# Attention scores, row maxima, window masks and layer-norm means issued as four column tiles of 32

## The reference, cut to what matters

```python
# layer 0, per image b, 4 heads of 16 channels
x_ln   = layernorm(x)                        # over the 64 channels
q,k,v  = split(einsum(x_ln, qkv_w))
scores = einsum(q, k) / sqrt(16)             # 1024 x 1024 per head
out    = softmax(scores) @ v
x      = x + proj(out)
x      = x + fc2(gelu(fc1(layernorm(x))))
# layer 1, per image, 8 heads of 64 channels, each token sees a window of 32 tokens
dot    = einsum(q1, windows_of(k1))
t      = t + softmax(dot) @ windows_of(v1) @ Wu
t      = t + scan(sigmoid(batchnorm(layernorm(t) @ W) + y @ V.T))
```

## Time and profile before

| what | us |
|---|---|
| median of 3 runs (lowest to highest) | 453.4 (451.02 to 453.89) |
| the profiled execution | 450.95 |
| its span, first to last instruction | 449.2 |
| PE busy, DVE busy, ACT busy | 410.0, 296.0, 296.4 |
| mean granted TensorE clock | 0.983 of 2.4 GHz |

### The profile page before, as it was taken

The page is one execution under the profiler, slowest core; times in us unless marked ns, Lnnn a source line. Parts: engine busy times, 40 slices in busy tenths (PEclk is TensorE's granted clock), DMA queues, the critical chain, the costliest instruction groups (busy, mean ns, idle before and its releaser), DMA issues.

```text
span 449.2 us, 7886 instructions
## 1 busy us (share of the span) xinstructions
PE 410.0 (91%) x3207; PEld 155.4 (35%) x3207; DVE 296.0 (66%) x541; ACT 296.4 (66%) x512; POOL 40.7 (9%) x55
## 2 busy tenths in 40 slices
PE   7789999999999999999999999899999888897893
PEld 2334323223223433333223333232234322453492
DVE  2698978989997646689986447996142635625424
ACT  3534777768786675796785684878976666164551
POOL 9100300002021000030040000000300001100000
PEclk9998999999999999999999999999999999699997
DMA  8400280004600000007200000000000000000003
GB/s 307 92 1 3 50 161 14 0 14 105 107 2 10 4 1 3 9 6 166 47 0 13 1 1 3 12 2 3 1 3 1 0 1 0 3 1 2 1 1 95
DMA packets 6942, 14.02 MB, mean 31 GB/s; under 512 B 1528, under 2 KB 4088, under 8 KB 6776
## 3 DMA queue, kind: packets, MB, share of 16 engines
q1 hardware_dynamic: 6760, 13.36, 12.7%
q10 hardware_dynamic: 144, 0.14, 0.1%
HBM read 9.20 MB, written 3.41 MB: 28 GB/s over the span
## 4 chain that ended last, share of the span: by engine, by line
PE 66%; ACT 18%; DVE 12%; issue 3%; DVEq 0%; ACTq 0%
PE O L828 11%; PE T L813 6%; DVE part_max L1318 5%; ACT z L1182 5%; PE T L793 5%; PE R L813 4%; ACT probs L1159 4%; PE R L793 4%; PE R L997 3%; PE R L958 3%; PE R L718 3%; PE R L724 3%; PE R L884 2%; PE R L985 2%; PE R L972 2%
## 5 line engine op out<-in xcount | busy, mean ns | idle before, releaser
L1318 DVE TENSOR_REDUCE part_max<-T 128x1 f32<-128x512 f32 x160 | 103.1, 681 | 16.7 <-PE T L793 16.3
L1159 ACT ACTIVATE probs<-T 128x512 f32<-128x512 f32 x151 | 84.4, 599 | 20.7 <-PE T L813 20.2
L1159 ACT ACTIVATE probs<-R 128x512 f32<-128x512 f32 x105 | 59.5, 601 | 20.1 <-PE R L813 19.5
L828 PE MATMUL O<-probs,VT 128*32 128x512 f32 x512 | 67.8, 603 | 0.4 <-ACT probs L1159 0.3
L1318 DVE TENSOR_REDUCE part_max<-R 128x1 f32<-128x512 f32 x96 | 62.8, 681 | 4.6 <-PE R L793 4.4
L793 PE MATMUL T<-KX,QX 96*128 96x512 bf16 x160 | 55.0, 387 | 4.4 <-DVE part_max L1318 2.1
L813 PE MATMUL T<-QX,KX 99*128 99x512 bf16 x151 | 51.8, 383 | 2.3 <-DVE part_max L1318 2.3
L813 PE MATMUL R<-QX,KX 99*128 99x512 bf16 x105 | 36.2, 382 | 0.0
L669 POOL CAST zs<-z 128x512 bf16<-128x512 f32 x28 | 17.4, 620 | 200.2 <-ACT z L1182 200.2
L793 PE MATMUL R<-KX,QX 96*128 96x512 bf16 x96 | 33.4, 384 | 1.2 <-DVE part_max L1318 0.7
L1190 ACT ACTIVATE p<-R 128x1024 f32<-128x1024 f32 x14 | 14.3, 1024 | 25.3 <-PE R L958 25.3
(11 more groups left out here) (240 smaller groups left out, 586.8 us busy)
## 6 DMA issues: line engine op xcount, KB each, us to landing
qk_scratch<-qk_part SPq DMA_DIRECT2D x12, 192.0 KB, 3.0
zs<-early SPq DMA_DIRECT2D x1, 2048.0 KB, 7.9
QX<-qk_scratch SPq DMA_DIRECT2D x6, 256.0 KB, 5.5
KX<-qk_scratch SPq DMA_DIRECT2D x6, 256.0 KB, 5.6
result<-probs SPq DMA_DIRECT2D x2, 512.0 KB, 5.1
s_rest<-rest SPq DMA_DIRECT2D x1, 946.0 KB, 10.9
X<-x SPq DMA_DIRECT2D x2, 384.0 KB, 12.5
QX<-qk_scratch SPq DMA_DIRECT2D x6, 128.0 KB, 5.4
```

Source lines behind the costliest of these rows:

```text
L828: last = mm(O[h * HP:(h + 1) * HP, :], VT[b % 2][:, j, h, :], probs[:, u % 2, h, :], start=(j == 0), stop=(j == KT - 1))
L1159: A(probs[:, u % 2, h, :], ring["scores", b, u, h], ACT.Exp, scale=HD ** -0.5).then_inc(g["exp_done"], 1)
L1318: nc.vector.tensor_reduce(part_max[:, row, kh:kh + 1], ring["max_piece", b, half, i], AX_X, ALU.max).then_inc(g["max_red"], 1)
```

## The change

A new function splits one matmul into four with 32 columns of weights each, all with the same moving operand, and gives the last one to the caller for its semaphore. Scores, maxima and the norms' two matmuls go through it. The window mask goes the same way, and its operand `win_mask` grows from 4 rows to 128, of which rows 4 to 127 are zero. The values and the windows' score matmuls stay as they are. No wait is added or removed.

```diff
-        win_mask = sb("win_mask", [TQ, UPB * 2 * GK + P], BF16)
+        win_mask = sb("win_mask", [P, UPB * 2 * GK + P], BF16)
...
+            def in_columns(bank, left, right):
+
+                for j in range(0, P, 32):
+                    last = mm(bank[j:j + 32, :], left[:, j:j + 32], right, start=True, stop=True)
+                return last
...
-                mm(ln_bank(b, which, i, 0), t["center"], ln_in(b, which, i), start=True, stop=True).then_inc(g["ln_ctr"], 1)
+                in_columns(ln_bank(b, which, i, 0), t["center"], ln_in(b, which, i)).then_inc(g["ln_ctr"], 1)
...
-                mm(ln_bank(b, which, i, 1), t["mean_c"], ln_bufs(b, which, i)["ln_q"], start=True, stop=True).then_inc(g["ln_var"], 1)
+                in_columns(ln_bank(b, which, i, 1), t["mean_c"], ln_bufs(b, which, i)["ln_q"]).then_inc(g["ln_var"], 1)
...
-                mm(ring["max_piece", b, half, i], QX[b % 2][0:KQ, half, h, nt * P:(nt + 1) * P], KX[b % 2][0:KQ, kh, h, :],
-                   start=True, stop=True).then_inc(g["max_mm"], 1)
+                in_columns(ring["max_piece", b, half, i], QX[b % 2][0:KQ, half, h, nt * P:(nt + 1) * P], KX[b % 2][0:KQ, kh, h, :]).then_inc(g["max_mm"], 1)
...
-                mm(ring["scores", b, u, h], KX[b % 2][:, j // QT, h, j % QT * P:(j % QT + 1) * P], QX[b % 2][:, half, h, :],
-                   start=True, stop=True).then_inc(g["st_mm"], 1)
+                in_columns(ring["scores", b, u, h], KX[b % 2][:, j // QT, h, j % QT * P:(j % QT + 1) * P], QX[b % 2][:, half, h, :]).then_inc(g["st_mm"], 1)
...
-                    mm(bank[:, 0:UPB * 2 * GK], win_mask[:, UPB * 2 * GK:], win_mask[:, 0:UPB * 2 * GK], start=True, stop=False)
+                    for gi in range(NG):
+                        rows = slice(gi * 32, (gi + 1) * 32)
+                        mm(bank[rows, 0:UPB * 2 * GK], win_mask[:, UPB * 2 * GK:][:, rows], win_mask[:, 0:UPB * 2 * GK], start=True, stop=False)
...
-                nc.vector.tensor_copy(win_mask[:], t["window_mask"][0:TQ, :])
+                nc.vector.tensor_copy(win_mask[:], t["window_mask"])
```

More of the change, by code:

```diff
@@ L162 @@
     (
-        0, 0, 1, 1, 2, 3, 4, 4, 6, 7, 7, 7, 7, 10, 10, 13, 13, 15, 16, 18, 18, 18, 18, 18, 18, 18, 18, 25, 29, 29, 33),
+        0, 0, 0, 1, 1, 1, 2, 3, 5, 5, 5, 8, 9, 10, 10, 12, 14, 15, 17, 17, 17, 20, 20, 23, 23, 23, 24, 26, 28, 32, 33),
     (
-        39, 39, 39, 43, 47, 48, 48, 48, 50, 51, 51, 53, 53, 53, 53, 55, 55, 61, 61, 61, 63, 64, 65, 65, 65, 66, 70,
-        72, 73, 73, 73, 76, 77, 79, 79),
-    (
-        80, 80, 80, 82, 82, 82, 84, 85, 86, 86, 86, 86, 97, 101, 101, 102, 102, 103, 103, 103, 105, 105, 105, 105,
-        105, 106, 107, 107, 107, 107, 107, 107, 108, 112, 112),
@@ L170 @@
-    (
-        112, 114, 114, 114, 114, 114, 115, 115, 116, 117, 117, 118, 121, 123, 125, 125, 127, 127, 134, 134, 135, 136,
-        137, 137, 137, 138, 143, 145, 146, 146, 146, 147, 148, 149, 149),
-    (
-        150, 152, 155, 156, 156, 163, 164, 164, 165, 168, 169, 170, 171, 171, 173, 173, 173, 173, 182, 184, 185, 185,
-        185, 186, 186, 186, 187, 187, 187, 189, 190, 190, 191, 192, 192),
-    (
-        192, 192, 193, 193, 193, 195, 195, 195, 195, 195, 195, 196, 196, 196, 197, 197, 198, 198, 199, 200, 211, 217,
-        217, 217, 217, 217, 221, 221, 224, 229, 229, 231, 233, 234, 235),
@@ L179 @@
-    (
-        238, 238, 239, 239, 240, 240, 240, 242, 243, 243, 243, 243, 253, 254, 256, 257, 257, 257, 257, 258, 258, 258,
-        261, 261, 262, 262, 263, 265, 266, 266, 266, 266, 266, 271, 271),
+        37, 38, 38, 38, 39, 39, 42, 45, 46, 48, 48, 49, 50, 52, 54, 55, 56, 58, 58, 60, 60, 62, 63, 65, 65, 67, 67,
+        72, 72, 73, 75, 76, 79, 79, 79),
+    (
+        80, 80, 80, 82, 83, 83, 85, 86, 86, 86, 86, 86, 97, 99, 99, 100, 100, 100, 100, 100, 104, 104, 104, 105, 105,
+        106, 107, 107, 107, 107, 107, 107, 107, 111, 113),
@@ new lines @@
+    (
+        113, 113, 114, 114, 114, 115, 116, 116, 116, 117, 117, 120, 121, 125, 125, 128, 128, 128, 128, 135, 136, 137,
+        137, 137, 138, 138, 143, 146, 146, 146, 146, 146, 146, 151, 155),
+    (
+        156, 157, 157, 158, 163, 166, 167, 167, 167, 168, 168, 169, 171, 172, 173, 173, 173, 173, 183, 183, 185, 185,
+        185, 186, 186, 186, 186, 188, 188, 189, 189, 189, 190, 191, 192),
+    (
+        192, 192, 192, 193, 193, 195, 195, 195, 195, 196, 196, 197, 197, 197, 197, 197, 199, 199, 199, 206, 210, 218,
+        219, 220, 220, 220, 225, 225, 229, 229, 229, 230, 230, 235, 236),
@@ L182 @@
+    (
+        238, 239, 239, 240, 240, 240, 241, 241, 243, 243, 243, 244, 252, 253, 257, 257, 257, 257, 257, 257, 258, 258,
+        262, 262, 263, 265, 265, 266, 266, 266, 267, 267, 270, 275, 279),
 )
 LAYER_AT = (
[10 rows of a table removed]
[10 rows of a table added]
 )
 END_AT = (
-    214, 215, 218, 218, 220, 221, 221, 222, 225, 227, 227, 229, 229, 231, 231,
+    214, 216, 217, 217, 220, 221, 222, 222, 225, 227, 227, 228, 229, 230, 231,
 )
 UNIFY_AT = (
-    278, 278, 278, 278, 282, 283, 284, 285, 286,
+    278, 278, 278, 278, 282, 282, 283, 284, 286,
```

## The result

The changed kernel takes 449.64 us in the median of 20 runs (446.24 to 453.68), the kernel before 452.16 in 20 runs beside it (449.64 to 455.01). The ratio is 0.9939, 95% interval 0.9922 to 0.9956: some 2.8 us less by the ratio, 2.5 between the two medians, where 11 were forecast. The profiled execution took 450.99 us; its mean granted clock is 0.976, where most runs have 0.982 to 0.989.

The account below looks back on a forecast made before the run. PE was taken to bound the kernel. Terms -13.0 + 1.6 - 1.2 + 1.3 = -11.3 us took 450.95 to 439.65; 1.2 for the profiled execution's low time gave 440.8 us, range 434 to 450.

Parts of the forecast that it names:

- What bounds the kernel: In the 64 units PE sets the time, busy 288.7 of 300 us; DVE close behind only in the first stretch.
- Shape changes, 134 x 0.097 us: On PE, changes of tile shape between neighbouring matmuls fall from 316 to 182: 13.0 us less.
- A group of four costs as one: Scores and maxima: four 32-column matmuls take 0.216 us, like one full-width matmul, when following their like.
- a group that pays 0.024 us: Rival, scores and maxima: every group costs 0.024 us more, +12.3 us in all; 450 to 453, chance 0.07.
- slow issue: Rival, runs of scores and maxima: load-matmul pairs cannot be issued at 54 ns; at 66 ns 465 us; chance 0.06.
- tiles that do not run at once: Rival, groups of four: tiles reading the same rows run serially, at least 0.216 us more each, over 550 us; chance 0.01.
- The term of +1.6 us for first groups: 65 scores, maxima, masks or norms following another shape pay 0.024 us each.
- the 16 weight loads of a window bank: Window scores: loads of different tiles overlap, all 16 lying within the 0.14 us of their matmuls.
- What is late next: DVE in the first image, pushed to 92% busy; a tenth of the 13.0 us lost to waits, +1.3 us.
- PE's gain becomes others' waits: Rival, ring of banks and DVE: half of the 13.0 us lost, +6.5 us; 445 to 447, chance 0.14.
- 434 to 450: Whole kernel: range covering the forecast's own 435 to 446, the half-lost case and the edge of the 0.024 us rival.
- The new places: New tables take shape changes from 193 to 182, 11 fewer; 3 us for better places at the range's low end.

Follow-up runs that it names:

- the best kernel: New tile shapes with the four old tables of places and the queries' and keys' loads split, against the kernel before: 444.14 us, ratio 0.9816.
- a lighter DVE: Changed kernel with maxima reductions reading 256 of 512 columns: 442.2 us, 0.9789; the same edit in the kernel before: 444.92 us, 0.9830.
- the old order: New tile shapes with the four old tables of places, against the kernel before: 446.99 us, 0.9893; with the loads split too, 444.14 us, 0.9816.
- the split loads: Changed kernel with keys and first half of the queries loaded first, second half's queries last: 447.02 us, ratio 0.9883 to the kernel before.
- one row back: Changed kernel with the second row of `MAX_AT` as before (second image's maxima begin at 39, not 37): 449.36 us, ratio 0.9928 to the kernel before.
- lighter exponentials: Exponentials over 256 of 512 columns, besides light reductions and no keys' wait: changed kernel 439.39 us, 0.9698; kernel before 446.35 us, 0.9853.

## Why the prediction was wrong, point by point

**What bounds the kernel.** Right for the units: PE set their time, and where it does not wait for a transfer it still does (271.83 of 285.20 us in the best kernel). But the reading looked at engines alone. The transfer of the second image's keys was hidden by PE's pace with no margin (landed at about 68.6, first used at 68.67). Neither the matmuls' waits nor the busy shares show a transfer that arrives in time by a hair; the row of the weight loads' waits, which does, was not read.

**Shape changes, 134 x 0.097 us.** The size of one and their count were right: the 0.10 us are gone wherever two matmuls now have one shape, and 0.10 to 0.12 stay where they have not.

**A group of four costs as one.** Right: 0.218 us a group, 0.86 us for the values, 0.25 for a window bank. The rivals of a group that pays 0.024 us, of slow issue and of tiles that do not run at once are all refuted by these rows. The term of +1.6 us for first groups was too large: behind another shape 0.226 us pass from a group to the next, behind its like 0.219 (medians of 50 and 317 places in the profile after), which makes 0.5 us. One reading was loose: the 16 weight loads of a window bank take 0.19 us and not 0.14, so they start within the time of their matmuls and do not end in it.

**What is late next.** This is the step that failed. It named DVE in the first image and took 1.3 us for all such waits. The runs showed in its place: the second image's keys, 3.5 us in the median (0.9939 against 0.9862 without the wait), and 4.1 us of standing still with 2.65 us of half clock behind it in the profiled execution. The waits for DVE's reductions stayed at 5 us, and in the kernel as it is a lighter DVE gave the change nothing. The rival "PE's gain becomes others' waits" was the right one in kind, but it was priced at 6.5 us and laid on DVE and the banks; of the 12.6 us that the other terms add up to some 10 went. That 449.64 us still lie inside 434 to 450 is luck: that edge was there for groups that each pay 0.024 us, which they do not.

**The new places.** The prediction took their numbers as worth 11 changes of shape, and 3 us more at the low end of the range. They begin the second image's maxima two places sooner, and with the keys where they are that costs: 0.9939 with them, 0.9893 without. The keys are not all of it: with the old shapes the new places cost 4.6 us (456.8), and the longest wait for the keys in that profile is 1.2 us. What else they cost was not taken apart.

**The rest.** With no wait for the keys the old order has 123 changes of shape fewer, 11.9 us by the price above, and 8.3 came in the medians, some of them by the clock. Among the units, where all but a few of the 123 stand, it was 6.6 us in the profiles: PE's busy time falls by 9.4 us (281.18 to 271.83), and its idle time grows from 10.6 to 13.4. Behind the last unit 13 changes fewer show no gain beside the clock's; PE is busy there for 81.86 of 103.90 us only. The grown idle time lies in many waits, most under a microsecond. DVE's reductions do not hold it, for with lighter ones it grows as well (11.4 to 15.6). ACT's exponentials were tried in vain, since transfers came in between, and the second layer's hand-overs were not tried. What holds the rest stays open.

## What to carry to other kernels

Where an engine is to become faster, look in the trace of before for every transfer whose landing lies just before its first use: it costs nothing there, hardly shows among the waits, and can be the next bound. A change of TensorE's tile shape cost about 0.1 us each time in this kernel, and matmuls that alternated with column-tiled ones could be cut into the same tiles at no cost for themselves. A new order of work has to be measured apart from the change that it comes with. Two kernels that differ by 1 or 2% are compared stretch by stretch, with the granted clock of each stretch beside it.

## What the runs showed of the hardware

A pause of PE can cost twice: behind the 4.1 us without a matmul the granted clock was 0.50 (1.2 GHz) for the next 5.3 us, with PE busy all the time. It does not do so each time: behind the wait of 2.5 us in the old places it was 0.50 for 3.4 us, from 69.6, but behind the 2.4 us with the split loads and the 2.5 us with one row back it stayed at 1.00.

With more instructions a transfer came later. Between the issue of the second image's four stores to `qk_scratch` and that of the first load, which waits for them, the kernel before took 5.2 us and the changed one 6.1. The issues of the queue before:

```profile
52.30 2.62 SPq L591 DMA_DIRECT2D qk_scratch<-qk_part  x4
57.48 0.35 SPq L603 DMA_DIRECT2D QX<-qk_scratch  x1
```

and after:

```profile
52.86 3.88 SPq L591 DMA_DIRECT2D qk_scratch<-qk_part  x4
58.92 0.35 SPq L603 DMA_DIRECT2D QX<-qk_scratch  x1
```

The view of the transfers after, from 52 to 60 us, has in it one packet of the instruction fetch, 0.02 MB:

```profile
q1 hardware_dynamic: 842, 0.83, 41.8%
q8 instruction: 1, 0.02, 1.1%
```

In the nine profiles with the new shapes and PE's larger program (without the two of lighter exponentials) the stretch took 5.9 to 6.3 us, in the five with the old shapes 5.1 to 5.2; the nine have a fetch packet in it, the five none. The store packets' own durations are the same (58 ns in the mean before, 59 after); after, it is the third store whose issue takes 1.88 us where the others take 0.6. That the fetch is the cause is argued from this and was not tried by itself; it would be 0.9 us of the 2 us by which the keys came later.
